# A decoder layer on one core: the cross-attention's PSUM banks, the slot of the query projection and the slots of the next rows' loads

## What is computed

```python
q = (x @ Wq).reshape(B, N, HEADS, hd).transpose(0, 2, 1, 3)        # 16 heads of 32
k = (context @ Wk).reshape(B, M, HEADS, hd).transpose(0, 2, 1, 3)
v = (context @ Wv).reshape(B, M, HEADS, hd).transpose(0, 2, 1, 3)
scores = jnp.where(context_mask, jnp.einsum('bhid,bhjd->bhij', q, k) * scale, max_neg)
out = jnp.einsum('bhij,bhjd->bhid', softmax(scores), v)
return out.transpose(0, 2, 1, 3).reshape(B, N, DIM) @ Wo
```

## Time and profile before

| | us |
|---|---|
| median of 3 executions | 3462.8 |
| lowest and highest of them | 3455.0, 3467.64 |
| the profiled execution's own time | 3456.58 |
| its span in the trace | 3454.8 |
| PE busy | 3183.5 (92%) |
| mean granted clock of PE | 0.971 of full |

### The profile page before, as it was taken

One profiled execution on the slowest core, in us unless ns is written; L12 is line 12 of the kernel. 1 busy time (PEld: TensorE's weight loads), 2 busy tenths in 40 slices (PEclk: granted clock), 3 DMA queues, 4 the chain that ended last, 5 costly groups with the idle time before them and its releaser, 6 DMA issues.

```text
span 3454.8 us, 47183 instructions
## 1 busy us (share of the span) xinstructions
PE 3183.5 (92%) x15056; PEld 2500.8 (72%) x15056; DVE 2618.3 (76%) x4327; ACT 2257.6 (65%) x4127; POOL 1098.4 (32%) x1192
## 2 busy tenths in 40 slices
PE   5999999999999999978999999988989999942998
PEld 4878888888888888865666666655778888731887
DVE  5987878787877777767888888887854379888564
ACT  4886767676776767655777777775432256678665
POOL 1233242333333333354666656666400000000000
PEclk9999999999999999989999999999999999975999
DMA  3453444434434433346666666655622268989764
GB/s 123 164 162 119 129 148 125 134 119 150 121 127 138 138 116 122 110 134 119 125 107 117 127 121 120 121 111 181 219 83 106 104 230 300 336 337 406 267 239 176
DMA packets 273028, 555.49 MB, mean 161 GB/s; under 512 B 28024, under 2 KB 105856, under 8 KB 259472
## 3 DMA queue, kind: packets, MB, share of 16 engines
q1 hardware_dynamic: 268560, 544.08, 52.6%
q10 hardware_dynamic: 4224, 8.39, 0.6%
HBM read 322.72 MB, written 162.30 MB: 140 GB/s over the span
## 4 chain that ended last, share of the span: by engine, by line
PE 33%; DMA 9%; DVE 6%; issue 3%; SPq 2%; ACT 2%; POOL 1%; ACTq 0%; POOLq 0%; DVEq 0%
PE gu_acc L2637 7%; DMA gu_g<-gate 3%; DMA ca_q<-ca_ql 3%; PE md_acc L2723 3%; PE md_acc L2724 3%; PE md_acc L2725 3%; PE ca_mx L2551 2%; PE ca_pj L2533 2%; PE ca_ov L2581 2%; PE ca_ov L2582 2%; PE ca_st L2569 2%; PE ca_ms L2541 2%; PE ca_pj L2522 1%; DMA gu_w_raw<-in_L_ffn_w_up_dram 1%; DMA md_ab<-up 1%
## 5 line engine op out<-in xcount | busy, mean ns | idle before, releaser
L915 POOL TENSOR_SCALAR sa_ex<-sa_ex,sa_rs 128x512 f32<-128x512 f32 x512 | 357.1, 697 | 906.0 <-DVE sa_rs L741 906.0
L736 DVE TENSOR_REDUCE sa_nm<-sa_st 128x1 f32<-128x512 f32 x512 | 350.3, 684 | 223.5 <-PE sa_st L1057 219.7
L578 ACT ACTIVATE sa_eh<-sa_tr 128x512 fp32r<-128x512 f32 x512 | 306.6, 599 | 293.4 <-PE sa_tr L1067 291.6
L1008 PE MATMUL sa_pj<-sa_xh,sa_w 128*128 128x512 f32 x1536 | 455.8, 416 | 3.0 <-DVE sa_xl L714 1.5
L2127 DVE TENSOR_REDUCE ca_negm<-ca_mx 128x1 fp32r<-128x512 f32 x512 | 344.9, 682 | 71.5 <-PE ca_mx L2551 69.0
L745 DVE TENSOR_TENSOR sa_el<-sa_tr,sa_eh 128x512 fp32r<-128x512 f32 x512 | 351.2, 686 | 41.0 <-ACT sa_eh L578 34.2
L571 ACT ACTIVATE sa_ex<-sa_st,sa_nm 128x512 f32<-128x512 f32 x512 | 351.3, 686 | 43.5 <-DVE sa_nm L736 39.5
L2420 POOL TENSOR_TENSOR ca_el<-ca_ex,ca_eh 128x512 fp32r<-128x512 f32 x256 | 358.4, 1405 | 42.9 <-ACT ca_eh L1916 41.3
L1908 ACT ACTIVATE ca_ex<-ca_st 128x512 f32<-128x512 f32 x512 | 298.3, 586 | 54.7 <-PE ca_st L2569 54.4
L1067 PE MATMUL sa_tr<-top_ident,sa_ex 128*128 128x128 f32 x2048 | 306.8, 272 | 1.8 <-POOL sa_ex L915 1.8
L1067 PEld LDWEIGHTS sa_tr<-top_ident,sa_ex 128*128 128x128 f32 x2048 | 254.3, 140 | 70.8 <-POOL sa_ex L915 4.3
(11 more groups left out here) (309 smaller groups left out, 7561.9 us busy)
## 6 DMA issues: line engine op xcount, KB each, us to landing
sa_w<-w_split SPq DMA_DIRECT2D x56, 1536.0 KB, 7.5
gate<-gu_ev SPq DMA_DIRECT2D x24, 1024.0 KB, 4.4
gu_g<-gate SPq DMA_DIRECT2D x48, 512.0 KB, 6.4
gate<-gu_g SPq DMA_DIRECT2D x48, 512.0 KB, 3.7
up<-gu_ev SPq DMA_DIRECT2D x24, 1024.0 KB, 5.7
md_ab<-gate SPq DMA_DIRECT2D x96, 256.0 KB, 6.5
md_ab<-up SPq DMA_DIRECT2D x96, 256.0 KB, 7.0
md_ab<-gate SPq DMA_DIRECT2D x44, 512.0 KB, 12.2
```

The source lines that it names most:

```text
L578: nc.scalar.activation(eh[:, v % ER], tr[:, v % 2], ACT.Copy).then_inc(act_eh, 1)
L736: nc.vector.tensor_reduce(nm[:, u % U:u % U + 1], st[:, u % 2], AX_X, ALU.max, negate=True).then_inc(dve_mx, 1)
L915: nc.gpsimd.tensor_scalar(ex[:, u % U], ex[:, u % U], rs[:, u % U:u % U + 1], 1.0, ALU.mult, ALU.mult).then_inc(pool_n, 1)
L1008: yield nc.tensor.matmul(pj[:, bank], w[:, n % 2, m, part, k], xx[b % 2][:, k], start=(i == 0 and k == 0), stop=(i == 2 and k == DK - 1))
```

## The change

1. `ov` becomes two banks: `ov0` for the even heads of a group and `ov1` for the odd ones. A head's first product waits for the emptying of the head before the last, not of the last.
2. `pj` becomes one bank, used by keys and queries in turn: the query projection waits until `km` of the same group has been read out, the key projection until `ql` of the group before has.
3. The queries move by one slot: their matmuls to t = 4 to 7, `qh` to t = 8, `ql` and `stack_queries` to t = 9.
4. The next rows' high part is loaded in t = 10 instead of 7, mask and low part in t = 12 instead of 9.
5. In the output projection the odd accumulator is `ms` instead of `pj[:, 1]`, and the odd transposes go to `ov0` instead of `ms`, with waits to fit.

```diff
-    KPASS, QPASS = (3, 3, 3), (0, 0, 0, 3, 3, 3, 3)
+    KPASS, QPASS = (3, 3, 3), (0, 0, 0, 0, 3, 3, 3, 3)
...
-            pj = bank("pj", [P, 2, S])
+            pj = bank("pj", [P, S])
+            ov0 = bank("ov0", [P, S])
...
-            ov = bank("ov", [P, S])
+            ov1 = bank("ov1", [P, S])
             ms = bank("ms", [P, S])
+            ov = (ov0, ov1)
...
-        acc = lambda j: pj[:, 1] if j % 2 else mx[:, 0]
-        pt = lambda j: ms if j % 2 else mx[:, 1]
+        acc = lambda j: ms[:, :] if j % 2 else mx[:, 0]
+        pt = lambda j: ov0 if j % 2 else mx[:, 1]
...
-                if t == 7 and s >= 0 and s % XG == 1 and s // XG + 1 < B:
+                if t == 10 and s >= 0 and s % XG == 1 and s // XG + 1 < B:
                     load_x(s // XG + 1, 0)
...
                 if t == 8 and n < N:
                     stack_keys(n)
+                if t == 9 and n < N:
                     stack_queries(n)
...
-                if t == 9 and s >= 0 and s % XG == 1 and s // XG + 1 < B:
+                if t == 12 and s >= 0 and s % XG == 1 and s // XG + 1 < B:
                     load_mask(s // XG + 1)
                     load_x(s // XG + 1, 1)
...
-                nc.scalar.activation(osb[:, j], ov[0:VW, :], ACT.Copy).then_inc(act_ov, 1)
+                nc.scalar.activation(osb[:, j], ov[j % 2][0:VW, :], ACT.Copy).then_inc(act_ov, 1)
...
-                if t == 7 and n < N:
+                if t == 8 and n < N:
                     high_query(n)
...
-                if t == 8 and n < N:
+                if t == 9 and n < N:
                     low_query(n)
...
                 if n:
-                    e.wait_ge(dve_km, n)
+                    e.wait_ge(dve_ql, n)
...
-                if n:
-                    e.wait_ge(dve_ql, n)
+                e.wait_ge(dve_km, n + 1)
...
-                    if a:
-                        e.wait_ge(act_ov, a // NT)
+                    if a >= 2 * NT:
+                        e.wait_ge(act_ov, a // NT - 1)
...
+                if i == 1:
+                    bank_free()
...
                 elif j == 1:
-                    bank_free()
+                    e.wait_ge(act_ov, HS * N - 1)
...
-                    if t == 3:
+                    if t == 4:
                         work["q"] = query_projection(n)
```

More of the change, by code:

```diff
@@ L1889, in high_query @@
                 e.wait_ge(pe_q, n + 1)
-                nc.scalar.activation(qh[:, :], pj[:, 1], ACT.Copy).then_inc(act_qh, 1)
+                nc.scalar.activation(qh[:, :], pj[:, :], ACT.Copy).then_inc(act_qh, 1)
             def high_value(j):
@@ L2109, in masked_key @@
                     e.wait_ge(pool_kl, n)
-                nc.vector.tensor_tensor(km[:, :], pj[:, 0], maskb[:, :], ALU.mult).then_inc(dve_km, 1)
+                nc.vector.tensor_tensor(km[:, :], pj[:, :], maskb[:, :], ALU.mult).then_inc(dve_km, 1)
             def low_query(n):
@@ L2115, in low_query @@
                     e.wait_ge(stacked[(n - 1) % RING], STACKS * ((n - 1) // RING) + STACKS)
-                nc.vector.tensor_tensor(ql[:, :], pj[:, 1], f32(qh[:, :]), ALU.subtract).then_inc(dve_ql, 1)
+                nc.vector.tensor_tensor(ql[:, :], pj[:, :], f32(qh[:, :]), ALU.subtract).then_inc(dve_ql, 1)
             def low_value(j):
@@ L2215, in out_work @@
                     e.wait_ge(pe_rb, n + 1)
-                    nc.vector.tensor_tensor(osum[:, n % SUM], osum[:, n % SUM], pj[:, 0], ALU.mult).then_inc(dve_o, 1)
+                    nc.vector.tensor_tensor(osum[:, n % SUM], osum[:, n % SUM], pj[:, :], ALU.mult).then_inc(dve_o, 1)
                 j = i - 1
@@ L2518, in key_projection @@
                 if n:
-                    e.wait_ge(dve_km, n)
+                    e.wait_ge(dve_ql, n)
                 for i, (w, part) in enumerate(((w_hi, 0), (w_lo, 0), (w_hi, 1))):
                     for k in range(CK):
-                        yield nc.tensor.matmul(pj[:, 0], w[:, k, cols(n % XG)], xc[:, part, k],
+                        yield nc.tensor.matmul(pj[:, :], w[:, k, cols(n % XG)], xc[:, part, k],
                                                start=(i == 0 and k == 0), stop=(i == 2 and k == CK - 1))
@@ L2532, in query_projection @@
                     for k in range(DK):
-                        yield nc.tensor.matmul(pj[:, 1], w[:, 2 * CK + k, cols(g)], xq[:, part, k],
+                        yield nc.tensor.matmul(pj[:, :], w[:, 2 * CK + k, cols(g)], xq[:, part, k],
                                                start=(i == 0 and k == 0), stop=(i == 2 and k == DK - 1))
@@ L2577, in product @@
                     e.wait_ge(dve_vl, NT * b + NT)
-                    if a:
-                        e.wait_ge(act_ov, a // NT)
+                    if a >= 2 * NT:
+                        e.wait_ge(act_ov, a // NT - 1)
                 values = vc[b % 2][:, kt, HS * g + h]
-                nc.tensor.matmul(ov[0:VW, :], values, eh[:, a % EL], start=(kt == 0), stop=False)
-                nc.tensor.matmul(ov[0:VW, :], values, el[:, a % EL], start=False, stop=(kt == NT - 1)).then_inc(pe_av, 1)
+                nc.tensor.matmul(ov[h % 2][0:VW, :], values, eh[:, a % EL], start=(kt == 0), stop=False)
+                nc.tensor.matmul(ov[h % 2][0:VW, :], values, el[:, a % EL], start=False, stop=(kt == NT - 1)).then_inc(pe_av, 1)
             def out_product(i):
@@ L2618, in spread_reciprocals @@
                     e.wait_ge(dve_ql, N)
-                nc.tensor.matmul(pj[:, 0], cast_r[:, :], rc[:, n % 2], start=True, stop=True).then_inc(pe_rb, 1)
+                nc.tensor.matmul(pj[:, :], cast_r[:, :], rc[:, n % 2], start=True, stop=True).then_inc(pe_rb, 1)
             def u_transposes(i):
```

## The result

The changed kernel takes 3469.6 us (median of 19 runs) against 3460.6 for the kernel of before on the same chip: a ratio of 1.0028, interval 1.0022 to 1.0035. One of the 19 took 8590 us with a mean granted clock of 0.5 of full, and the ratio leaves it out. The changed kernel is slower by 9 us, where 7 us less were forecast: a difference smaller than the 0.5% that the prediction called no change, but clear of noise here, and on the other side of zero. The profiled execution took 3466.15 us by its own time, its span is 3464.4 us (before: 3456.58 and 3454.8).

What follows compares the result with a forecast made beforehand. PE, busy in 92% of the span, was taken as the bound, with DVE full in two stretches. The terms 1 - 1.2 + 5 + 1.3 + 1.5 - 0.5 gave 7.1 us less, put at 3456 us, range 3435 to 3473.

Steps and rivals of the forecast that it cites:

- fourth part: Later loads of next rows and mask: stack waits of 8.3 us go, 3 given back at km, 5 us gained.
- third rival: Loads share the queue; stack's wait stays or masks are 1 us later per batch: 5 to 8 us worse, 3463; chance 0.2.
- Ring order: Skill's rule applied to loads behind the stack: they take nothing from it, 8.3 us go for certain; sum the same.
- First part: Two ov banks: osb waits go but mostly return as negm waits, since DVE is full; 1 us gained.
- Second part: One bank for keys and queries: about 0.15 us km wait a group, lost in eight s % 4 = 3 groups; 1.2 us lost.
- second rival: km becomes the gate of every group at t = 4: wait 1.0 us a group, 3487; chance 0.12.
- Third part: Queries' stack issued one slot later on SP, about 1.5 us, covered by the keys' transfers; costed at nothing.
- Fifth part: Ends of the loop: 1.3 us gained behind the split of Wo, 1.5 in osb waits, 0.5 lost at the start.

Runs made afterwards that it cites:

- e1: Changed kernel with the next batch's mask loaded in t = 10, ahead of the rows' high part, instead of t = 12: 3466.9 us, ratio 1.0026.
- e11: Changed kernel without the row loads of batches 1 to 7 and their waits; all batches use batch 0's rows: 3447.8 us, ratio 0.9962.
- e13: Changed kernel with the rows' high part in slot 7 behind the eighth query matmul, mask and low part in slot 9: 3456.7 us, ratio 0.9979.
- e4: e1 with the old wait back, a head's first product waiting for the emptying of the head just before: 3468.9 us, ratio 1.0025.
- e8: e5 with the head's product ahead of the query matmuls in t = 4: 3461.7 us, ratio 1.0007.
- e2: Changed kernel with the loads back in t = 7 and t = 9, old semaphore kept: 3468.8 us, ratio 1.0027.
- e12: Changed kernel with the mask loaded in slot 7 ahead of the key stack, rows still in slots 10 and 12: 3468.9 us, ratio 1.0017.
- e9: Changed kernel with high part in slot 7 behind the eighth query matmul, mask and low part in slot 9, product first in t = 4: 3450.8 us, ratio 0.9973.
- e5: Changed kernel with the rows' high part in t = 8 between keys' and queries' transfers, mask and low part in t = 9: 3465.9 us, ratio 1.0022.
- e10: Kernel of before with the rows' high part issued in slot 6 behind the eighth query matmul, instead of slot 7: 3463.7 us, ratio 1.0010.
- e7: Kernel of before with both halves of the rows issued from ACT's queue, mask in t = 7 on SP: 3496.9 us, ratio 1.0111.

## Why the prediction was wrong

**The fourth part failed, and with it the sign.** Its sentence was "The same bytes stay ahead of the mask, so it lands as before". It took 5 us gained, net, where kind 2 shows 12.3 lost (some 2.4 of them by the clock). The stack's wait did go (7.3 us, all of it), and was paid for twice over: PE waits 15.8 us for `km`, not some 3. Two things were wrong in the step. Counting bytes took the queue for a pipe of one speed, though rows 11 already had two: 110 to 160 for the plain stack and 180 to 210 with rows ahead. The prediction read the second as "loads run beside the stack", where from 1715.6 on it was the stack's own pace. And the step never set the mask's issue, now at t = 12 behind a whole stack at 130 GB/s, against the slot that wants it, t = 3 of the next group: 7 slots for it, where there had been 10.

The third rival named this place (the masks "later by 1 us in every batch: 5 to 8 us worse", 3463) with 0.2. It was the right place at half its size: 1.9 us at landing on average, and about 2 of wait in each batch. That the rows' place costs the time, and not the mask's own, is shown by e1, e11 and e13; why the stack runs faster behind the rows is not.

**Ring order.** Issued behind the stack, the rows took nothing from it: its slices read 108 to 151, where a group without loads reads 113 to 164. The Trainium skill's rule ("DMA: Bandwidth & Descriptors", "Queues, rings and completion order": on each engine descriptors are consumed in ring order) agrees with this trace. But the order set the pace as well, and the sum had no term for that.

**First part, low in size, and its cause in doubt.** `osb` is gone and waits for `negm` come up to 9.1 us in 29 ("over 12" was expected). 1 us was taken; kinds 0 and 1, where DVE is full, gave 0.8 + 3.3. By e4 the bank gives only 0.6 of that. It saves 3.2 in kind 3, which the old wait would have cost with the moved queries, and the prediction had neither. Nor was DVE's busy time a bound: with the product moved too (e8), a light group takes 0.36 us less than before, where 0.09 was said to be there.

**Second part.** In groups of kind 3 the loss is 171.5 - 170.3 = 1.2 us, the number summed, but in part by luck. The second rival, `km` as the gate of every group, did not come: the time lost there is 0.25 us a group: 0.15 ahead of the first query matmul, as expected, and 0.10 behind it. e8 shows that it was avoidable, and that kinds 0 and 1 lost 1.7 and 2.0 us by it too, where the prediction had it made up.

**Third part.** Nothing lost, as costed: no stack wait in 700 us. The premise was off: `ql` was issued 0.3 us later in light groups and 1.0 in kind 3, not 1.5.

**Fifth part.** The start, up to the first cut, lost 0.7 us (0.5 expected). The end gained 0.5, not 2.8: behind the split of Wo the wait only passes to the next scores, and in the whole loop's list they now have a wait of 6.1 us for `ex`, where `osb` had 6.2.

**The terms together:** forecast 1 - 1.2 + 5 + 1.3 + 1.5 - 0.5 = +7.1; measured 0.8 + 3.3 - 1.2 - 12.3 + 0.5 - 0.7 = -9.6. Of the 16.7 us between them the fourth part holds 5 + 12.3 = 17.3; the first was 3.1 better, the ends 2.5 worse. The kinds are sorted by where the time was lost, not by which edit lost it, so the single terms are rough.

## What to carry to other kernels

A transfer moved out of the way of one consumer must be followed to its own: write down for each when it lands behind what is now ahead and when it is wanted, and take the rate for that from the stretch in which it will run. Where a move looks right but a wait comes back under another name, look for the semaphore that forces the late issue; here a buffer was free four matmuls before its semaphore said so, and a finer one alone took the ratio from 1.0027 to 0.9979 (e2, e13), 17 us. And check by the granted clock of each stretch what a single profile says of a few us.

## What the runs showed that was not expected

- The stack of keys and queries goes at 105 to 174 GB/s alone or behind 256 KB (e12), at 184 to 213 or 138 to 265 (e9) behind 1 MB of rows, and at 108 to 167 again when that megabyte is in its middle (e5). Why is open. That the DMA engines fall out of step behind the long load, and so stop meeting at the same place, would fit, but nothing here shows it: the single packets are faster (145 to 191 ns against 262 to 275), and the profile doesn't tell the engines apart.
- Why the early rows help in e9, issued 0.9 us before the stack, and hurt in e10, issued 2.2 us before it, is open too. The stack's stretch shows it: 196 to 237 GB/s in the seven batches of e9, and 168 to 205 in six of e10's, where the kernel before had 180 to 234.
- With the rows on a second queue PE waits up to 6.0 us a batch for the stack (e7), where it waits up to 1.9 with the high part ahead of it on one queue. e7 moves both halves of the rows at once, and the clock fell in each of its batches, so the difference is not the price of the queue alone.
